# Group attention on one Trainium2 core: the value products of all positions summed by TensorE with the identity, where VectorE summed them

## The reference, cut to what matters

```python
# hidden_states: (S=8, B=512, 128)
ln1 = _ln(hidden_states, ln1_weight, ln1_bias)
qkv = (ln1 @ qkv_weight.T).reshape(S, B, N_KV, (Q_PER_KV + 2) * HEAD_DIM)
q, k, v = ...                       # k and v are repeated for the two query heads of a pair
scores = einsum('sbhd,tbhd->bhst', q, k) / sqrt(HEAD_DIM)
attn = softmax(where(causal, scores, NEG), axis=-1)
attn_out = einsum('bhst,tbhd->sbhd', attn, v).reshape(S, B, H)     # the change is in this sum over t
hidden_after_attn = hidden_states + attn_out @ proj_weight.T
x = _ln(hidden_after_attn, ln2_weight, ln2_bias)
probs = softmax(x @ router_weight)  # then top 2 of 8 experts, rows scattered to the experts
```

## Time and profile before

| what | us |
|---|---|
| three timed runs | 976.47 median (974.27 to 980.98) |
| the profiled execution, its own time | 976.01 |
| its span in the profile | 974.3 |
| mean granted TensorE clock | 0.942 |
| busy in the span: PE, DVE, ACT, POOL | 825.0, 695.1, 552.2, 557.4 |
| stage D, from the first row normed to the first expert matmul | about 525 to 795 |

### The profile page before, as it was taken

One profiled execution on the slowest core, in us unless ns is written; L12 is line 12 of the kernel. 1 busy time (PEld: TensorE's weight loads), 2 busy tenths in 40 slices (PEclk: granted clock), 3 DMA queues, 4 the chain that ended last, 5 costly groups with the idle time before them and its releaser, 6 DMA issues.

```text
span 974.3 us, 18283 instructions
## 1 busy us (share of the span) xinstructions
PE 825.0 (85%) x6646; PEld 542.3 (56%) x6646; DVE 695.1 (71%) x1441; ACT 552.2 (57%) x1027; POOL 557.4 (57%) x617
## 2 busy tenths in 40 slices
PE   7789998999899999999996877679788859999870
PEld 4356664448644444444443645445556549988870
DVE  5889984014798999999975599988576853654573
ACT  6566665440488887878884743436786544343220
POOL 2500006807188888888332599962077735878872
PEclk9899999999999999999998988789999979999995
DMA  5012210237021211121202992001011021232296
GB/s 160 1 44 87 87 44 23 65 130 206 13 44 37 30 30 35 35 36 35 35 14 62 167 285 84 1 1 43 1 48 53 28 94 43 89 99 65 89 247 206
DMA packets 109897, 70.62 MB, mean 72 GB/s; under 512 B 41538, under 2 KB 103436, under 8 KB 108272
## 3 DMA queue, kind: packets, MB, share of 16 engines
q1 hardware_dynamic: 99440, 60.11, 24.4%
q0 software_dynamic: 4608, 6.64, 2.1%
q10 hardware_dynamic: 5760, 2.70, 1.0%
HBM read 32.04 MB, written 31.60 MB: 65 GB/s over the span
## 4 chain that ended last, share of the span: by engine, by line
PE 37%; DVE 27%; POOL 13%; issue 10%; ACT 3%; DMA 2%; ACTq 1%; SPq 0%; POOLq 0%; DVEq 0%
PE banks L1975 5%; POOL y_dram L947 4%; DVE B_mneg L1122 4%; PE banks L1944 3%; PE banks L1921 3%; PE banks L1962 3%; PE banks L1894 3%; PE banks L1888 2%; DVE D_dmx L1238 2%; DVE C_nmax L1060 2%; PE banks L2045 2%; PE banks L1866 2%; PE banks L1949 2%; PE banks L2096 2%; PE banks L2003 2%
## 5 line engine op out<-in xcount | busy, mean ns | idle before, releaser
L1122 DVE TENSOR_REDUCE B_mneg<-banks 128x2 f32<-128x768 f32 (+1 forms) x128 | 136.4, 1086 | 7.7 <-PE banks L1949 4.0
L1637 ACT ACTIVATE B_pt<-banks 128x768 f32<-128x768 f32 (+1 forms) x128 | 117.1, 917 | 31.2 <-PE banks L1962 29.3
L785 POOL TENSOR_SCALAR_AFFINE_SELECT B_pt<-B_pt 128x512 f32<-128x512 f32 x128 | 80.4, 636 | 82.4 <-ACT B_pt L1637 62.6
L1768 ACT ACTIVATE F_gh<-banks 128x512 f32<-128x512 f32 (+1 forms) x96 | 49.4, 527 | 87.0 <-PE banks L2165 83.0
L902 POOL DMA_INDIRECT rows_dram<-F_xs,F_rowi x64 | 62.5, 977 | 59.6 <-issue 59.0
L1975 PE MATMUL banks<-B_pt,B_vp 128*32 128x512 f32 (+3 forms) x1024 | 95.6, 444 | 0.5 <-POOL B_pt L785 0.2
L2096 PE MATMUL banks<-D_qk 128*128 128x512 f32 x128 | 75.8, 677 | 10.2 <-DVE D_pr L1249 10.2
L947 POOL DMA_INDIRECT y_dram<-F_yo,F_ide x60 | 59.9, 998 | 37.8 <-DVE F_yo L1466 17.3
L2173 PE MATMUL banks<-F_gw,F_gh 128*128 128x128 f32 x640 | 75.3, 275 | 0.2 <-DVE F_yo L1466 0.2
L2173 PEld LDWEIGHTS banks<-F_gw,F_gh 128*128 128x128 f32 x640 | 73.9, 192 | 1.1 <-DVE F_yo L1466 0.4
L1944 PE MATMUL banks<-B_kt,B_qt 64*128 64x256 bf16 (+3 forms) x512 | 72.7, 301 | 1.7 <-ACT B_pt L1637 1.2
(11 more groups left out here) (300 smaller groups left out, 2228.3 us busy)
## 6 DMA issues: line engine op xcount, KB each, us to landing
comb_dram<-C_comb SPq DMA_DIRECT2D x6, 1024.0 KB, 3.9
rows_dram<-D_zeros SPq DMA_DIRECT2D x8, 650.0 KB, 15.5
F_xe<-rows_dram SPq DMA_DIRECT2D x8, 650.0 KB, 3.9
C_w<-w_in SPq DMA_DIRECT2D x16, 256.0 KB, 3.0
C_cst<-comb_dram SPq DMA_DIRECT2D x4, 1024.0 KB, 7.0
y_dram<-D_zeros SPq DMA_DIRECT2D x2, 2048.0 KB, 17.7
F_gw<-mw_in SPq DMA_DIRECT2D x16, 256.0 KB, 3.2
F_xs<-y_dram SPq DMA_DIRECT2D x16, 256.0 KB, 5.1
```

The costliest lines, as they stand in the source:

```text
L785: g.affine_select(out=w, in_=w, compare_op=ALU.is_ge, fill=0.0, base=0, pattern=[[0, G], [1, P]], channel_multiplier=-1).then_inc(B_md, 1)
L1122: v.tensor_reduce(mneg[:, g % 2, :, pairs[0], qt_], scores[:, :, 0:w], X, ALU.max, negate=True).then_inc(B_mx, 1)
L1637: a.activation(pt[:, 2 * hp:2 * hp + 2, PT_AT[kt]:PT_AT[kt] + w], scores[:, :, 0:w], ACT.Exp).then_inc(B_ex, 1)
```

## The change

POOL writes the products of a position n as slabs of 128 columns, one for each seen position t, where it wrote the seen positions of one column beside each other. The inner loop still runs over t, so that neighbouring writes now lie 512 bytes apart (they lay 4 bytes apart). The shapes, the operands read and the number of instructions on POOL stay.

The DVE function `group_outputs` goes away. A new PE function `sum_values` takes its place in the same order: for each n it waits for the same semaphores and does s+1 accumulating matmuls with the identity as the stationary operand, each over one slab of 128 columns, into the same columns of the same PSUM bank. That is 18 matmuls for a group, 144 in all. `group_done` waits for them as it waited for DVE's sums.

```diff
@@ POOL, group_values
-                        prodv[:, off:off + w].rearrange("p (g k c t) -> p g k c t", t=s_ + 1, g=2, c=HD)[:, gg],
+                        prodv[:, off:off + w].rearrange("p (t g k c) -> p g k c t", t=s_ + 1, g=2, c=HD)[:, gg],
@@ DVE
-            def group_outputs(k, n):
-                s_ = SEEN[k % 2][n]
-                off = P * sum(c + 1 for c in SEEN[k % 2][:n])
-                if n == 0:
-                    ...
-                dve.wait_ge(D_pv, 8 * k + 2 * n + 2)
-                v.tensor_reduce(misc_bank(D_PLAN.nth("misc", "N", k, 0))[:, n * D:(n + 1) * D], prodv[:, off:off + (s_ + 1) * P].rearrange("p (c t) -> p c t", c=P),
-                                X, ALU.add).then_inc(D_gr, 1)
...
-                elif kind == "gw":
-                    group_outputs(a_, n)
@@ PE
+            def sum_values(k, n):
+                s_ = SEEN[k % 2][n]
+                first = sum(c + 1 for c in SEEN[k % 2][:n])
+                if n == 0:
+                    old = D_PLAN.back("misc", ("N", k, 0), 3)
+                    if old[0] in D_BY_ACT:
+                        pe.wait_ge(D_ma, D_PLAN.nth("act", *old))
+                    else:
+                        pe.wait_ge(D_md, D_PLAN.nth("dve", *old))
+                pe.wait_ge(D_pv, 8 * k + 2 * n + 2)
+                for t in range(s_ + 1):
+                    ins = t_.matmul(misc_bank(D_PLAN.nth("misc", "N", k, 0))[:, n * D:(n + 1) * D], ident[:],
+                                    prodv[:, (first + t) * P:(first + t + 1) * P], start=(t == 0), stop=(t == s_))
+                ins.then_inc(D_gr, 1)
...
+                elif kind == "gw":
+                    sum_values(a_, n)
```

## The result

The changed kernel takes 980.06 us (median of 20 runs, 978.51 to 984.77) against 976.51 for the kernel before (20 runs beside them, 974.27 to 981.72). The ratio is 1.0043, with a 95% interval of 1.0031 to 1.0055: slower by 0.4%. That is within 1%, the case with the largest chance, and inside the range, but the forecast was 0.5% faster (971.5 us), and the sign is wrong. That the time lies inside the range is owed to the range's width and not to the sum, as the part on why the prediction was wrong shows. The profiled execution took 980.41 us, with a span of 978.7 us.

A forecast was written before the change was run, and what follows sets the result against it. DVE and POOL were taken as full in the group attention, with POOL's 96.7 us busy time as floor. POOL's gaps closing by 3.7 and 0.8 us took 4.5 us off 976.0, giving 971.5 us; range 963 to 984.

The forecast's parts named there:

- the case with the largest chance: Whole kernel: the time stays within 1% of the kernel before, chance 0.64.
- Two engines are full, and the change relieves one: Group attention: DVE busy 99.0 of 108.1 us falls to about 79.4; POOL's 96.7 us stays as the floor.
- The price of a matmul: PE's new sums: 0.22 us a matmul at full clock, 0.43 at half; 32 or 62 us for all 144.
- The clock stays up in the groups: PE in the group attention: the new matmuls fill gaps that lowered its clock, leaving each group 1.8 us ahead.
- POOL's writes cost nothing: POOL's products: writing 512 bytes apart adds nothing, as reads set the pace; upper bound 17.0 us.
- the second rival: POOL's products: writes 512 bytes apart are slower, by up to 17.0 us, giving 988 us; chance 0.11.
- POOL's gaps: POOL's waits in groups 6 and 7: 0.82 and 2.89 us vanish, 7.27 shrinks to 6.5; together 4.5 us gained.
- PE has room: PE in the group attention: 68 us of full-clock work plus 32 new make 100, fitting the 108.1 us stretch.
- The end of group 7: 4.1 us before and after: From POOL's last product to the scaled output's end: 4.15 us before, about 4.1 after, so no gain.
- The other streams shift with it: Rest of the stage and behind: an earlier end of the groups shifts everything, so the gain passes on at full value.
- PE becomes the bound: Group attention: at a mean clock of 0.83 PE needs 120.8 us, 13 us longer, giving 989 us; chance 0.12.

The follow-up runs named there:

- exp7_early: Changed kernel with the exponential of group 7 put earlier on ACT: 980.64 us, ratio 1.0042 to the kernel before.
- exp7_two_buffers: Changed kernel with the exponential of group 7 earlier on ACT and a second buffer for POOL's products: 978.91 us, ratio 1.0021 to the kernel before.
- last_two_old_layout: Changed kernel, but DVE sums groups 6 and 7, which POOL writes in the layout of the kernel before: 973.55 us, ratio 0.9964 to the kernel before.
- half_sums: Changed kernel with 80 of the 144 sum matmuls, every second seen position left out (wrong result): 973.85 us, ratio 0.9996 to the kernel before.
- clock_filler: Changed kernel with four idle matmuls of 512 columns in PE's wait for the first normed rows: 978.10 us, ratio 1.0028 to the kernel before.
- double_sums: Changed kernel with every sum on PE done twice, 288 matmuls, same result: 1011.07 us, ratio 1.035 to the kernel before.

## Why the prediction was wrong, point by point

- **Two engines are full, and the change relieves one: held.** DVE fell to 80.8 us (79.4 forecast), POOL kept its 96.3 us (33.92 + 40.51 + 21.83; 96.7 forecast).
- **The price of a matmul: held.** 36 records take 4.18 us at 605.73 and at 665.55, 0.23 a matmul (0.22 forecast). That is at full clock; behind the 4.02 us wait 20 records (10 matmuls) took 3.05 us.
- **The clock stays up in the groups: held,** 1.00, 0.96 and 0.95 against 0.90, 0.75 and 0.85 in the earlier trace rows. The wait of 3.99 us ahead of group 3's turn is gone. This turn was walked through to 614 us and came at 612.77, and the projection behind the three pieces that follow came at 616.37 where 617.4 was forecast: 2.8 us ahead instead of 1.8. (The prediction takes the three half-speed pieces as costing 2.6 us; its rows make it 4.98 - 2.65 = 2.3.)
- **POOL's writes cost nothing: held,** 1530 against 1522 ns, and the second rival falls with it. The reason given, that the product's pace is set by its reads, fits but was tested by no run.
- **POOL's gaps: two right, the third wrong.** The 0.82 and 2.89 us are gone. The 7.27 us was to shrink to 6.5 and became 10.26. The step left out that POOL comes to this gap earlier by the gaps removed ahead of it (at 649.20 instead of 653.15, 3.95 us) while the exponential, on ACT behind score tiles of PE, came only 1 us earlier. And two things stood behind it which it didn't see: the single product buffer (exp7_early), and that the gap was no longer on the path (exp7_two_buffers).
- **The failed step is "PE has room", 68 + 32 = 100 us in a stretch of 108.** It was worked out as a mean over the whole stretch. The room that could be used was ahead of the pause of 4 us in which PE waits for DVE's output of a b; behind it there was none. The same sum on that part alone, with the row of before shown above, would have told: 16.49 us at a clock of 0.83 are 13.7 us of full-clock work, and the 36 matmuls of groups 6 and 7 add 7.9, which makes 21.6 us for a stretch of 18.04. The measured stretch is 23.47, of which 22.74 busy at a clock of 0.93, 21.1 of full-clock work. The experiments show that this is the cause: the same stretch, from the end of the pause to the turn of group 7, takes 18.01 us with no matmul of sums in it (last_two_old_layout), 20.01 with 20 (half_sums), 23.47 with 36 (after; 24.6 to 24.7 in exp7_early, exp7_two_buffers and clock_filler, where half speed lasts longer behind the pause) and 32.71 with 72 (double_sums). So the lead of 4.3 us, nearly the 4.5 of the forecast, was there at 649.6, and was spent by 673.
- **"The end of group 7: 4.1 us before and after" was mis-sized.** From the last product (666.7) to the turn (673.06) it is 6.4 us; before it was 4.3 (667.65 to 671.95). All 18 matmuls of the group stand behind 665.55, since PE came to them late; the prediction had 11 of them done while POOL still worked. And it counted a turn and a score tile behind the sums, where PE has another turn, a product and another score tile as well ahead of the turn of group 7, 2.2 us (670.87 to 673.06).
- **"The other streams shift with it" did not hold in the trace.** The clock fell behind the groups (0.62 against 0.91), for 2.4 of the 3.55 us. In exp7_early and exp7_two_buffers, with the same sums on PE, it held: 35.9 us from the turn to the first scatter against 36.08.
- **The rival "PE becomes the bound" was the right mechanism,** but on the wrong condition (a clock under 0.92) and so 9 us too dear: the clock was 0.97 from 559.0 to 666.7, and PE still was the bound, in the last sixth of the stretch. double_sums shows the same mechanism in full.

## What to carry to other kernels

When work moves to an engine that "has room", work out the room for each part between two of its long waits, not over the stage: the room in front of a wait that another engine ends is worth nothing behind it. A mixed assignment can beat both pure ones, here by 0.4% against the kernel before: TensorE sums the groups whose time is hidden, VectorE the last two, each in the layout that its engine reads well. And before a gap is called the path, look for the second thing that the waiting engine needs right after it.

## What the runs showed of the hardware that was not expected

POOL's `tensor_tensor` in f32 writes elements 512 bytes apart at the price of neighbours (1530 against 1522 ns for 512), though a memset of elements 128 bytes apart costs 0.92 ns more an element; DVE's `tensor_reduce` pays for the same distance on its reads, 1920 against 1220 ns for 1024 elements. And behind a pause of TensorE of 3.2 us half-speed rows followed in every trace without the filler, but for unequal times: they cost 0.9 us of path in some traces and 3.5 in others, held against the kernel in which four idle matmuls filled the pause.
